# Attention over paged keys: output products spread over the next group, one head in four transposed by DMA, new keys in one matmul a head

## What is computed

```
x = x + einsum('bct,bcd->bdt', x, weights[subjects])
q, k, v = x @ Wq.T, x @ Wk.T, x @ Wv.T          # q and k: rmsnorm, then rotation by position
k_all = concat([k_cache[block_table], k], axis=1)   # 512 old keys, 32 new ones
v_all = concat([v_cache[block_table], v], axis=1)
scores = einsum('bqhd,bkhd->bhqk', q, repeat(k_all, 4)) * SCALE, masked beyond cache_seqlens
o = einsum('bhqk,bkhd->bqhd', softmax(scores), repeat(v_all, 4))
out = x + einsum('bse,de->bsd', o.reshape(b, s, 32 * 128), Wo)
```

## Time and profile before

| | us |
|---|---|
| median of 3 runs | 1045.36 (1040.63 to 1048.02) |
| the profiled execution | 1046.1 |
| its span | 1044.3 |
| TensorE busy | 982.7 (94%) |
| VectorE busy | 795.1 (76%) |
| ScalarE busy | 717.4 (69%) |
| GpSimd busy | 493.7 (47%) |

### The profile page before, as it was taken

The page is one execution under the profiler, slowest core; times in us unless marked ns, Lnnn a source line. Parts: engine busy times, 40 slices in busy tenths (PEclk is TensorE's granted clock), DMA queues, the critical chain, the costliest instruction groups (busy, mean ns, idle before and its releaser), DMA issues.

```text
span 1044.3 us, 24950 instructions
## 1 busy us (share of the span) xinstructions
PE 982.7 (94%) x8329; PEld 779.9 (75%) x8329; DVE 795.1 (76%) x1705; ACT 717.4 (69%) x1959; POOL 493.7 (47%) x642
## 2 busy tenths in 40 slices
PE   4889999999889999899999999998999999999998
PEld 2678888887678788769768857965976986895793
DVE  6779999999997788758847856865784885786680
ACT  4898999988765778747746746754774774675670
POOL 5445665566881266516415523622441641552340
PEclk9999999999999999999999999999999999999999
DMA  5789999989989899778998998999899999899740
GB/s 202 247 278 336 322 390 367 385 279 398 380 288 326 309 337 343 266 192 294 323 235 267 357 234 243 328 241 228 301 291 243 294 329 241 260 354 249 240 148 11
DMA packets 268016, 296.49 MB, mean 284 GB/s; under 512 B 94064, under 2 KB 225648, under 8 KB 265328
## 3 DMA queue, kind: packets, MB, share of 16 engines
q1 hardware_dynamic: 249200, 227.65, 71.3%
q0 software_dynamic: 18688, 67.25, 19.3%
HBM read 231.77 MB, written 46.27 MB: 266 GB/s over the span
## 4 chain that ended last, share of the span: by engine, by line
PE 54%; DVE 16%; SPq 8%; DMA 7%; issue 6%; ACT 5%; POOL 2%; ACTq 0%; DVEq 0%; POOLq 0%
PE ps_o L1411 16%; PE ps_proj L1411 15%; PE ps_o L1489 8%; SPq L640 5%; PE ps_s L1449 4%; PE ps_s L1453 4%; PE ps_t L1460 3%; DVE probs L1154 2%; DMA vs<-v_pages,v_row 2%; DMA kt<-k_pages_t 2%; PE ps_rt L1559 2%; DVE rot L1282 2%; DVE c_stage L1310 2%; PE ps_o L1503 1%; ACT probs L930 1%
## 5 line engine op out<-in xcount | busy, mean ns | idle before, releaser
L865 POOL TENSOR_SCALAR probs<-probs,recip 128x544 f32<-128x544 f32 (+1 forms) x256 | 157.5, 615 | 382.2 <-DVE recip L1162 377.7
L930 ACT ACTIVATE probs<-probs,neg_max 128x544 f32<-128x544 f32 x256 | 191.3, 747 | 155.5 <-DVE neg_max L1154 154.7
L1154 DVE CUSTOM_DVE_ANT_0 probs<-ps_s,mask,row_scale 128x544 f32<-128x544 f32 x256 | 200.1, 782 | 126.3 <-PE ps_s L1453 123.5
L1489 PE MATMUL ps_o<-pt,vs 128*128 128x128 f16 x3072 | 214.3, 220 | 8.2 <-DMA pt<-wo 3.8
L1489 PEld LDWEIGHTS ps_o<-pt,vs 128*128 128x128 f16 x3072 | 192.3, 98 | 19.0 <-issue 6.6
L821 POOL TENSOR_TENSOR roped<-rot 128x256 f32<-128x256 f32 x160 | 144.2, 922 | 82.2 <-DVE rot L1274 76.3
L1411 PE MATMUL ps_proj<-wt_hi,x0t_hi 128*128 128x512 f32 x384 | 159.7, 416 | 8.0 <-DVE x0t_lo L1112 7.0
L1411 PE MATMUL ps_o<-wo,ot_hi 128*128 128x512 f16 x512 | 153.7, 382 | 10.4 <-DVE ot_lo L1186 10.4
L1411 PE MATMUL ps_proj<-wt_hi,x0t_lo 128*128 128x512 f32 x384 | 151.7, 395 | 0.0
L1411 PE MATMUL ps_proj<-wt_lo,x0t_hi 128*128 128x512 f32 x384 | 150.8, 393 | 0.0
L853 POOL DMA_INDIRECT vs<-v_pages,v_row x128 | 131.4, 1026 | 22.3 <-issue 20.2
(11 more groups left out here) (146 smaller groups left out, 1599.0 us busy)
## 6 DMA issues: line engine op xcount, KB each, us to landing
kt<-k_pages_t SPq DMA_DIRECT2D x512, 128.0 KB
c_nat<-in_L_cond_k_cache SPq DMA_DIRECT2D x32, 512.0 KB, 5.8
q_t<-stage SPq DMA_DIRECT2D x64, 256.0 KB, 7.3
c_nat<-in_L_cond_v_cache SPq DMA_DIRECT2D x32, 512.0 KB, 7.2
qt<-q_t SPq DMA_DIRECT2D x32, 512.0 KB, 6.2
w_nat<-in_L_cond_Wq SPq DMA_DIRECT2D x8, 1024.0 KB, 8.9
k_pages_t<-c_stage SPq DMA_DIRECT2D x16, 512.0 KB, 5.8
c_nat<-in_L_cond_Wo SPq DMA_DIRECT2D x16, 512.0 KB, 7.7
```

The source lines that it names most:

```text
L865: pool.tensor_scalar(part, part, col(recip, i), 1.0, ALU.mult, ALU.mult).then_inc(p_norm, 1)
L930: act.activation(pr, pr, ACT.Exp, bias=col(neg_max, i), scale=-1.0, accum_out=col(row_sum, i)).then_inc(a_exp, 1)
L1154: dve.tensor_tensor_reduce(out=probs_of(i), in0=ps_s[:, score_cols(i):score_cols(i) + KEYS], in1=mask[(i // HK) % 2][:, mask_at(i):mask_at ...
L1489: ins = pe.matmul(ps_o[n % 2][:, jl * P:(jl + 1) * P], v[:, part, :], pt[i % NPT][:, NCH * half + c, :], start=jl == 0 and c == 0 and k == ...
```

## The change

1. **Output products.** `project_out` takes one head at a time (3 matmuls). Heads run from step r = -1 (the last step of the group itself) to r = 28 of the next group, one a step, two in steps 3 and 4. The last group takes 4, 6, 6 and 16 heads in its last step and the three behind it. They sum into a bank of their own, `ps_y`, which comes from the third `ps_t`: from step 28 on two banks hold the transposes. `add_residual` runs once a group.
2. **Layout of the context.** `ot_hi` and `ot_lo` are no longer one block a head. In odd groups the 128 columns of a head lie 32 elements (64 bytes) apart, in even groups 8 elements (16 bytes), so that a finished quarter of the products frees the place of one batch. ScalarE and VectorE read `ps_o` in a strided order for it and write pieces of 16 or 8 elements. In even groups the rows of residual and output are permuted by the DMA.
3. **Transposes by DMA**: from step 39 on each head with i mod 4 = 3, 55 in all.
4. **SyncE's order**: for each batch one DMA transpose; queries, edge keys and 6 pages for the batch after next; the second DMA transpose; the other 10 pages and the new values.
5. **New keys.** Rows are high, low and high part again (96 rows), values high, high, low; no padding. One matmul a head, 4 instead of 8 in `weigh_new`. The third block of probabilities is copied by GpSimd (`tn_copy`), ScalarE and VectorE now take two instructions of 32x256 each where one of 64x256 stood, in the step of the transposes. The values come by 3 DMAs of 256-byte pieces.

```
-    ptn = [sb(f"ptn{i}", [4 * SEQ, 2, P], F16) for i in range(2)]
+    ptn = [sb(f"ptn{i}", [3 * SEQ, 2, 2, P], F16) for i in range(2)]
-    NTB = 3
+    NTB = 2
+    ps_y = psum("ps_y", [P, HID])
-    STEPS = NP2 + 2 * HPC + 3
+    STEPS = NP2 + HPC
-    TN, TNE, OE = HPC - 1, HPC, HPC + 2
-    DMA_FIRST, DMA_LAST, STAGED = 2, 11, 3
+    TN, TNE, TNC, OE = HPC - 1, HPC - 1, HPC, HPC + 2
+    DMA_FIRST, STAGED, T_THIRD = 39, 3, 28
     def by_dma(i):
-        return 0 < i < NP2 and g >= 1 and (DMA_FIRST if g > 1 else 8) <= r <= DMA_LAST
+        return DMA_FIRST <= i < NP2 and i % HPC == HPC - 1
+    Y_AT = {r: (r + 1,) for r in range(-1, 3)} | {3: (4, 5), 4: (6, 7)} | {r: (r + 3,) for r in range(5, HQ - 3)}
+    Y_LAST = {-1: range(0, 4), 0: range(4, 10), 1: range(10, 16), 2: range(16, HQ)}
+    def head_tokens(tile, g, n):
+        if g % 2 == 1:
+            return tile[:].rearrange("p (m h) -> p m h", h=HQ)[:, :, n]
+        k, j = divmod(n, QUARTER)
+        return tile[:].rearrange("p (k m j) -> p k m j", k=GB, j=QUARTER)[:, k, :, j]
...
-            PAGES_IN = {5: 0, 6: 4, 7: 8, 0: 12}
+            AHEAD_OF_TURN = 6
+            for b in range(B):
+                turn_last(HK * b + HPC - 1)
+                if b + 2 < B:
+                    load_queries(b + 2)
+                    load_pages(b + 2, 0, AHEAD_OF_TURN)
+                turn_last(HK * b + HK - 1)
+                if b + 2 < B:
+                    load_pages(b + 2, AHEAD_OF_TURN, NPP - AHEAD_OF_TURN)
+                    load_new_v(b + 2)
...
+            def tn_copy(n, normed):
+                pool.wait_ge(a_tnhi, n + 1)
+                pool.wait_ge(p_norm, normed)
+                pool.tensor_copy(ptn[n % 2][2 * SEQ:3 * SEQ], ptn[n % 2][0:SEQ]).then_inc(p_tncopy, 1)
+                pool.wait_ge(p_tncopy, n + 1)
...
             def weigh_new(n):
+                pe.wait_ge(p_tncopy, n + 1)
                 pe.wait_ge(v_tnlo, n + 1)
-                for m in range(2):
-                    for e in range(2):
...
+                for jl in range(HPC):
+                    m, e = divmod(jl, 2)
+                    ins = pe.matmul(ps_o[n % 2][:, jl * P:(jl + 1) * P], vn[b % 2][:, HPC * h + jl, :],
+                                    ptn[n % 2][:, e, m, :], start=False, stop=jl == HPC - 1, skip_group_check=True)
...
+                hi, lo = head_tokens(ot_hi, g, n), head_tokens(ot_lo, g, n)
+                ins = products(ps_y[:], [(hi, wo[:, h, 0, :]), (hi, wo[:, h, 1, :]), (lo, wo[:, h, 0, :])],
+                               first=n == 0, last=n == HQ - 1)
```

More of the change, by code:

```diff
@@ L558, in evacuated, with context @@
             eng.wait_ge(v_tnlo, i + 1)
+    def context(n):
+        return ps_o[n % 2][:].rearrange("p (h t) -> p t h", t=SEQ if n // NBG % 2 == 1 else NHALF * SEQ)
     def all_stored(eng):
@@ L1395, in _ @@
                     row_recip(i + 2)
-                if at(i, OE) is not None and y_part(i) is None:
+                if at(i, OE) is not None:
                     ot_lo_of(at(i, OE))
```

192 lines of the change are left out of this document (92 added, 100 removed).

## The result

The changed kernel takes 1095.7 us (median; 1084.0 to 1102.5) where the kernel before takes 1046.0 in the same runs: ratio 1.045, 95% interval 1.035 to 1.054. Ratios are of fast runs alone, since a kernel's executions fall into a faster and a slower state; times in brackets are the lowest and the highest of all runs. The prediction was 1020, in 1004 to 1036. It is wrong in sign and outside its range.

The account below looks back on a forecast made before the run. PE was taken to bound the kernel, busy 982.7 of 1044.3 us. 1046.1 - 8.3 (PE work) - 33.5 (idle) + 3 (banks) + 4 (before 434 us) + 10 (transposes, operands, pauses) = 1021.3, less 0.7: 1020; range 1004 to 1036.

Parts of the forecast that it names:

- the term for SyncE and the DMA transposes: SyncE's queue: late transposes cost between 0 and 62 us; taken near the median landing, +6 us.
- The leads: Time from a transpose's issue to its need by PE: 7.0 us behind six pages, otherwise 6.7, 4.6 in seven storing batches.
- The landing: Time a DMA transpose takes from its issue: 4.0 us in the median, 11.8 at most, 7.7 for the late one.
- One late one among 64: DMA transposes of the kernel before: this count, with the 4.0 us median, was the argument against the late-transposes rival.
- The rival of late transposes: SyncE's queue: transposes land later than before, each costing what exceeds its lead; 1030 to 1076 us, chance 0.12.
- The argument for the low value: DMA queue: the same bytes spread over a batch instead of bursts at 314 GB/s, so +6 us, near the median landing.
- Idle time for `ot_lo` and the result: PE's waits in the output product and for `add_residual` go; all idle time of PE was put at -33.5 us.
- Steps of 2.2 to 2.7: PE with one head of product a step: even steps, 2.46 us each, instead of 1.8 to 2.3 and 4 to 4.4.
- The third bank's price: Two banks for transposes: PE waits for `t_lo` in steps 31 and 35, some 1.5 us each, +3 us.
- The +4 for the stretch before 434 us: ScalarE and VectorE set the pace there; one instruction more for each of nine half batches, 0.42 us at most: +4.
- operands, +2: Stationary operands 16 and 64 bytes apart in the output product: 0 to 12 us, taken as 2.
- Strided stationary loads: Rival, output product: loads over 216 ns show in each matmul; 68 us at four times 98 ns, 1088; chance 0.07.

Follow-up runs that it names:

- e2_noturn: The changed kernel with its 55 DMA transposes left out, those heads weighed with the transposed probabilities of the head before: 1014.2 us, ratio 0.971 to the kernel before.
- e13_halfpages: The changed kernel with eight of the sixteen pages of each batch left out from the third on, three ahead of the second transpose: 1095.4 us, ratio 1.052.
- e8_newkeys: The kernel before with only the new keys in three blocks (part 5 of the change): 1061.7 us, ratio 1.017.
- e17_nogather: The changed kernel with the gathers of values left out from batch 4 on, all other loads and transposes kept: 1018.2 us, ratio 0.974.
- e15_early3: The changed kernel with pages in four paced portions, the last put early, heads weighed a step later, new values behind the first transpose: 1054.3 us, ratio 1.015.
- e7_behind4: The changed kernel with each head weighed two steps later (six pt buffers) and new values behind the first transpose: 1046.8 us, ratio 0.995.
- e18_early_gathers: The changed kernel with gathers two each in steps 8b+2 and 8b+3, a fifth pt, new values, output and residual behind the 8b+3 transpose: 1065.5 us, ratio 1.021.

## Why the prediction was wrong

**The failed step is the term for SyncE and the DMA transposes, +6, which is +81** (`e2_noturn`). Its pieces:

- *The leads.* For heads 8b+7 7.0 us were forecast and 7.3 measured. For heads 8b+3 it was 6.7, 4.6 in seven batches, and the median is 5.4, the lowest 2.7: a microsecond too long.
- *The landing.* The median of before, 4.0, was carried over to all. But it was a mixture (table above): 3.5 with no gather within 6 us ahead, 5.8 right behind one, where only 9 of 64 stood. In the changed kernel 40 of 55 stand there, with 7.6: of the 28 heads 8b+7, 24 are issued within 2.6 us behind a gather, and so are 16 of the 27 heads 8b+3, since the event that releases these is that of gather 1 too (`weigh` of head 8b-1 frees both `pt` and `vs`). The change made the bad case the rule.
- *Why before didn't suffer.* "One late one among 64" was taken as evidence of quick transposes. It was one of long leads: 12.5 us in the median, and the one that was late had the shortest of all, 4.0. Transposes of before and the `weigh` of the same heads:

```profile
515.64 1.82 SPq L754 DMA_TRANSPOSE pt<-wo  x1
519.97 2.80 SPq L754 DMA_TRANSPOSE pt<-wo  x2
520.25 1.02 POOL L853 DMA_INDIRECT vs<-v_pages,v_row  x1
522.28 1.01 POOL L853 DMA_INDIRECT vs<-v_pages,v_row  x1 [0.16 <-issue]
525.46 8.59 SPq L754 DMA_TRANSPOSE pt<-wo  x3
525.83 1.01 POOL L853 DMA_INDIRECT vs<-v_pages,v_row  x1 [0.16 <-issue]
...
527.17 0.83 PE L1489 MATMUL ps_o<-pt,vs 128*128 128x128 f16 x12
531.13 0.83 PE L1489 MATMUL ps_o<-pt,vs 128*128 128x128 f16 x12
535.89 0.83 PE L1489 MATMUL ps_o<-pt,vs 128*128 128x128 f16 x12 [0.20 <-issue]
540.06 0.83 PE L1489 MATMUL ps_o<-pt,vs 128*128 128x128 f16 x12
```

  The old kernel had its transposes in the steps with four heads of product, some 4.1 us each. From 515.64 to 527.17 are 11.5 us, for the following ones 11.2, 14.4 and 14.6. Landings of 10.8 and 11.8 us (leads 13.4 and 14.6) passed unseen. Spreading the product over all steps shortened each of these to 2.46 us: the lead fell to 5.4 and 7.3 us in the same change that moved the transposes beside the gathers. The prediction worked out the new lead and never the old one.
- *The price of a late one.* The rival of late transposes named what happened, with a chance of 0.12. It counted only what a landing is over the lead: 56 of the 81 us are that. Some 20 of the others are, by the estimate above, the clock behind a pause: 1.28 us for a head of product instead of 0.65. And it took one landing for all. It put 29 us on a usual landing of 7.1; 7.1 is the median that came, but spread from 2.8 to 10.4. So its 1030 to 1076 was too low; its bound of 7.7 us was below the 11.8 that rows 9 show.
- The argument for the low value, "over 9.83 x 2 us a batch instead of bursts", looked at pages. Halving them changed nothing (`e13_halfpages`). The four gathers of a batch, 2 MB like its pages, were not in the term at all.

**What held.** Idle time for `ot_lo` and the result: gone. Steps of 2.2 to 2.7: 2.45 measured. `weigh_new`: 602.03 to 602.26 = 0.23. The signs of being wrong: waits for `pt<-wo` over 10 us were named as the sign of late transposes, and they came, and so did 30 us of idle time in the last 600 (60.8 from 434 us on). The sum without the failed term: 1014 and 1014.2.

**Where that sum was lucky.** The third bank's price was put at +3. In `e2_noturn` PE waits 7.6 us for `t_lo` (8.2 in the changed kernel; 0.8 before), nearly all of it before 451 us. The +4 for the stretch before 434 us was right. Of before, and of the changed kernel:

```profile
424.55 0.83 PE L1489 MATMUL ps_o<-pt,vs 128*128 128x128 f16 x12
...
426.90 0.63 PE L1501 MATMUL ps_t<-fixed,probs 128*128 128x128 f32 x4 [1.98 <-DVE pt L1221]
434.81 0.38 PE L1509 MATMUL ps_t<-fixed,probs 128*64 128x128 f32 x2 [1.05 <-DVE pt L1221]
435.73 0.83 PE L1527 MATMUL ps_o<-pt,vs 128*128 128x128 f16 x12
```

The first and the last row are `weigh` in step 31. From the first `weigh` of all (361.12 and 365.24) to it are 63.4 and 70.5 us: 7.1 more, of which 3.0 are the two waits for `t_lo`, the bank's. The other 4.1 are of the new keys. So the bank cost some 3 us more than its term, and smaller terms (operands, +2, other pauses, +2) were too high by about as much. In the changed steps the new keys' added instructions are covered, as the steps of 2.45 us show; in tight ones they aren't (`e8_newkeys`).

**Strided stationary loads** cost no time that shows. PEld, against rows 10:

```profile
L1452 PEld LDWEIGHTS ps_y<-wo,ot_hi x510: 136/146/168, 440.3 to 1089.7; 128*128 128x128 f16 x170
```

146 ns instead of 98, alike for steps of 16 and of 64 bytes (medians of a group of heads 144 and 145 or 146), under matmuls 216 ns apart. A head of product takes 0.66 us in the median in all eight groups. By the Trainium skill, SBUF — State Buffer, "Door 1", a step of up to 8 two-byte elements is free and a longer one would pay. This trace agrees with neither half: both loads are half as long again as the contiguous one, and neither shows in the time.

**Open.** By which mechanism a gather delays a transpose. The 55 transposes move 58,080 packets (247,376 against 189,296 without them) of 14.4 MB, 248 bytes each; a gather's packets are 3.6 KB (67.25 MB in 18,688). In the example most of the delay lies ahead of the transpose's own packets: after the issue at 614.13 gather packets take 51.5% of the 16 engines' time until 618.4, with 94 packets under 512 bytes among 920, and 1,080 small ones follow by 622.2; it landed 2.0 us behind these, at 624.20. In `e17_nogather` a transpose issued at 592.57 has its 1,082 small packets from 593.4 to 596.1 and lands at 596.70. Small packets that stand behind large ones would fit this, and so would descriptors; neither was tried. Also open is why `e15_early3` has late transposes with no gather near, and why the late ones are later still from ScalarE's queue.

No kernel tried beats the one before by more than half a per cent with all its work in it (`e7_behind4`, 0.995). What `e17_nogather` and `e18_early_gathers` point to was not tried: gathers away from the transposes without a second one in a step of GpSimd, and a step more of lead.
